# First layer of a graph network: a gathered chunk's products between the counting slots, table products two slots later, normalisation between one-hots

## What is computed

```
norm = deg_inv_sqrt[row] * deg_inv_sqrt[col]
msgs = x[row] * norm[:, None]
x = layernorm(x + segment_sum(msgs, col))            # first layer
h = relu(edge_attr_32 @ W1 + b1); w = (h @ W2 + b2).reshape(e, 4, 8, 8)
x = layernorm(x + (sums over edges of products of x[src], edge_attr_4 and w) + x @ si)   # second layer
```

## Time and profile before

| what | value |
|---|---|
| time, three runs | 3489.55 us median (3487.09 to 3490.99) |
| the profiled execution | 3488.94 us, of which the span of its instructions 3486.2 us |
| VectorE busy | 2974.5 us (85%) |
| TensorE busy (products) | 2796.1 us (80%) |
| GpSimd busy | 2464.9 us (71%) |
| ScalarE busy | 1433.7 us (41%) |
| first gathers of the first layer, last one's end | 105.3 us, 1281.8 us |
| first gather of the second layer | 1312.5 us |

### The profile page before, as it was taken

The page is one execution under the profiler, slowest core; times in us unless marked ns, Lnnn a source line. Parts: engine busy times, 40 slices in busy tenths (PEclk is TensorE's granted clock), DMA queues, the critical chain, the costliest instruction groups (busy, mean ns, idle before and its releaser), DMA issues.

```text
span 3486.2 us, 55367 instructions
## 1 busy us (share of the span) xinstructions
PE 2796.1 (80%) x17493; PEld 1893.0 (54%) x17493; DVE 2974.5 (85%) x6514; ACT 1433.7 (41%) x3154; POOL 2464.9 (71%) x2520
## 2 busy tenths in 40 slices
PE   5699999999999987777777787777778777877775
PEld 4477776777777764444444454444445444444443
DVE  8788888888888865988888889889889888988987
ACT  0788888888888863211121112111212121112211
POOL 0677776777777657777777777777777777777774
PEclk9999999999999997999898898999989998999988
DMA  2200000000000021111111111111111111111112
GB/s 50 29 14 14 13 14 13 14 14 13 12 14 14 13 34 22 31 27 28 27 31 27 27 27 31 27 27 28 30 27 28 27 31 27 27 28 27 31 27 34
DMA packets 181444, 85.57 MB, mean 25 GB/s; under 512 B 124024, under 2 KB 167608, under 8 KB 181176
## 3 DMA queue, kind: packets, MB, share of 16 engines
q0 software_dynamic: 79872, 41.05, 8.0%
q1 hardware_dynamic: 101304, 41.07, 5.2%
HBM read 77.13 MB, written 4.81 MB: 24 GB/s over the span
## 4 chain that ended last, share of the span: by engine, by line
POOL 39%; issue 17%; ACT 17%; PE 14%; DVE 12%; DVEq 1%; DMA 1%; POOLq 0%; SPq 0%; ACTq 0%
POOL xg L435 39%; ACT z_sb L476 9%; ACT q_sb L476 7%; PE ps L635 4%; PE ps L648 4%; PE ps L593 3%; DVE prod_all L1062 2%; DVE stage L1231 2%; PE ps L623 1%; DVE oh L949 1%; DVE prod_all L1221 1%; PE ps L739 1%; DVE sumT_all L1085 1%; DVE lane L1058 1%; DVE z_sb L841 1%
## 5 line engine op out<-in xcount | busy, mean ns | idle before, releaser
L435 POOL DMA_INDIRECT xg<-x_table,idx x1664 | 1602.5, 963 | 562.7 <-issue 531.4
L435 POOL DMA_INDIRECT xg<-scaled_x_table,idx x832 | 854.9, 1028 | 400.7 <-issue 374.5
L739 PE MATMUL ps<-w2t,hT 128*128 128x256 f32 x3328 | 899.8, 417 | 283.9 <-DVE prod_all L1221 278.9
L739 PEld LDWEIGHTS ps<-w2t,hT 128*128 128x128 f32 x3328 | 643.2, 204 | 735.7 <-issue 640.3
L635 PE MATMUL ps<-prod_all,lane 128*128 128x363 bf16 (+1 forms) x2496 | 792.5, 320 | 51.8 <-DVE prod_all L1062 35.0
L1062 DVE TENSOR_SCALAR prod_all<-wide_lane,key 128x363 bf16<-128x363 bf16 (+1 forms) x2496 | 730.4, 316 | 27.8 <-PE ps L635 23.0
L1231 DVE TENSOR_REDUCE stage<-prod_all 128x192 f32<-128x1536 f32 x416 | 724.0, 1741 | 0.2 <-issue 0.2
L523 ACT ACTIVATE hT<-ps,b 64x512 f32<-64x512 f32 x416 | 284.4, 684 | 932.7 <-PE ps L732 928.6
L476 ACT ACTIVATE q_sb<-ps 128x363 bf16<-128x363 f32 (+1 forms) x1248 | 504.7, 543 | 94.2 <-PE ps L635 87.8
L476 ACT ACTIVATE z_sb<-ps 128x363 bf16<-128x363 f32 (+1 forms) x1248 | 504.7, 543 | 85.1 <-PE ps L635 81.8
L1215 DVE TENSOR_TENSOR prod_all<-ps,stage 128x768 f32<-128x768 f32 x416 | 397.1, 955 | 143.6 <-PE ps L739 68.7
(11 more groups left out here) (128 smaller groups left out, 1528.5 us busy)
## 6 DMA issues: line engine op xcount, KB each, us to landing
efT<-in_efT SPq DMA_DIRECT2D x104, 256.0 KB
xg<-x_table,idx POOLq DMA_INDIRECT x1664
xg<-scaled_x_table,idx POOLq DMA_INDIRECT x832
sh<-in_sh SPq DMA_DIRECT2D x104, 32.0 KB
idx<-in_src SPq DMA_DIRECT2D x156, 8.0 KB
scaled_x_table<-q_sb SPq DMA_DIRECT2D x2, 784.0 KB, 7.6
x_table<-x_sb SPq DMA_DIRECT2D x7, 224.0 KB, 4.7
out_rows<-q_sb SPq DMA_DIRECT2D x6, 224.0 KB
```

Of the source, the lines that this page charges most:

```text
L435: pool.indirect_dma_start(rows[k][:, t, :], None, table, bass.IndirectOffsetOnAxis(ap=idx[k][:, t:t + 1], axis=0),).then_inc(s_g[layer][k] ...
L739: mm = pe.matmul(ps_w[j % 2][:, t, :], hT[j % 2][:, t * P:(t + 1) * P], w2t[:].rearrange("p c o i -> p (c o i)"), start=True, stop=True)
```

## The change

- **Products woven in.** `window_sums` takes a list of tiles. TensorE makes one product of chunk n-1 after every second slot of turn n, in the first 32 slots; those of the last two chunks come after the loop, in blocks. `slots_until` now gives even numbers.
- **Slots in pairs, more buffers.** `count_tile` waits only at even slots, for the pair; there are 4 PSUM banks for counts in place of 3 and `KR` = 8 spread buffers in place of 7 (`LEAD` stays 6).
- **Table products two slots later.** `apply_counts` is cut into 13 shares (`SHARES`) in place of 16, in slots 2 to 14 of the next range.
- **VectorE's order.** In turn n: the spreads of the first 34 slots, `add_gathered(n - 1)`, `one_hots(n + 1)`, `scale`, then the other spreads. Where a group is centred, its six instructions stand between six cuts of these other spreads (`centre_step`), one turn after TensorE has made its rows. The table adds that are left stand after the loop, ahead of the last chunk's add, as before.
- **Rows of a group.** `sums_to_rows` also waits for one-hots (`hots`), and stands behind the next turn's slots.
- **Lanes.** The bank of the lanes is taken by the fourth count bank. 128 lanes go to the end of bank 7, used by the chunk's one-hots alone; the table one-hots read `near_lanes` from SBUF.

```diff
@@
 RANGES = 3
 HR = 33
 HB = 14
-KR = 7
-LEAD = KR - 1
+KR = 8
+LEAD = 6
+SHARES = 13
+SPAN_SLOTS = 2 * TPC
 GB = 14
+STEPS = 6
 SLACK = 40
 WIDE = 512
 D = 32
@@
     assert KEY0 + 2 * P <= RW
 
     def slots_until(n):
-        return min(SLOTS, -(-SLOTS * (n + 1) // (CG - 1)))
+        return min(SLOTS, -(-SLOTS * (n + 1) // (2 * CG - 2)) * 2)
 
     def last_chunk_of(g):
         return CHUNKS - 1 if g == NG - 1 else min(CHUNKS - 1, math.ceil((GB * P * (g + 1) + SLACK) / RISE) - 1)
@@
         ps_sum = [ps[0:m, 6, 0:SPC * SW].rearrange("p (s w) -> p s w", s=SPC) for m in (D, DM)]
         ps_rows = ps[:, 7, 0:GB * D]
         ps_wide = [ps[0:m, 7, :] for m in (D, DM)]
-        ps_ring = [ps[:, b, 0:RW] for b in range(3)]
-        ps_lanes = ps[:, 3, 0:LW // 2]
-        lanes = ps_lanes.bitcast(BF16)
+        ps_ring = [ps[:, b, 0:RW] for b in range(4)]
+        ps_lanes = ps[:, 7, GB * D:GB * D + P // 2]
+        span_lanes = ps_lanes.bitcast(BF16)[:, 0:SW]
         ps_dense = [ps[0:D3, 4 + b, 0:TPC * TWIN] for b in range(2)]
         ps_low = ps[:, 7, 0:P]
         ps_piece = [ps[:, 3 + j % 4, 0:HB * D] for j in range(HBS)]
...
@@
                         mm.then_inc(s_dmm, 1)
             pe.matmul(ps_deg, zero_b[:], zero_b[:, 0:NP], start=False, stop=True).then_inc(s_degree, 1)
 
-            def window_sums(layer, rows, n):
+            def window_sums(layer, rows, n, tiles=range(TPC)):
 
                 k = n % 2
-                if layer == 0:
-                    pe.wait_ge(s_g[0][k], 16 * TPC * (n // 2 + 1))
-                else:
-                    pe.wait_ge(s_msg, 2 * n + 2)
-                pe.wait_ge(s_oh[layer], n + 1)
-                if n >= 1:
-                    pe.wait_ge(s_acc[layer], SPC * n)
-                for t in range(TPC):
+                for t in tiles:
+                    if t == 0:
+                        if layer == 0:
+                            pe.wait_ge(s_g[0][k], 16 * TPC * (n // 2 + 1))
+                        else:
+                            pe.wait_ge(s_msg, 2 * n + 2)
+                        pe.wait_ge(s_oh[layer], n + 1)
+                        if n >= 1:
+                            pe.wait_ge(s_acc[layer], SPC * n)
                     mm = pe.matmul(ps_sum[layer][:, t // TPS, :], rows[:, t, :], oh[layer][k][:, t, :],
                                    start=(t % TPS == 0), stop=(t % TPS == TPS - 1))
-                mm.then_inc(s_sum[layer], 1)
+                    if t == TPC - 1:
+                        mm.then_inc(s_sum[layer], 1)
 
             def wide_sums(layer, rows, n, landed):
 
...
-            def sums_to_rows(layer, g, gathered, dense):
-
+            def sums_to_rows(layer, g, gathered, dense, hots=0):
+
+                if hots:
+                    pe.wait_ge(s_oh[layer], hots)
                 pe.wait_ge(s_acc[layer], SPC * gathered)
                 if layer == 0:
                     pe.wait_ge(s_dacc, TPC * dense)
@@
             def count_tile(s):
                 g, t = s // TPC, s % TPC
                 a, b = spread_hi[g % RANGES]
-                if g % RANGES == 0:
-                    pe.wait_ge(s_ohlow, g // RANGES * TPC + t + 1)
-                pe.wait_ge(s_spread, s + 1)
-                if s >= 3:
-                    pe.wait_ge(s_evict, s - 2)
-                pe.matmul(ps_ring[s % 3][:, 0:(b - a) * TWIN], ohlow[:, t, :], spread[s % KR][:, 0:(b - a) * TWIN],
+                if s % 2 == 0:
+                    pe.wait_ge(s_spread, s + 2)
+                    if g % RANGES == 0:
+                        pe.wait_ge(s_ohlow, g // RANGES * TPC + t + 2)
+                    if s >= 4:
+                        pe.wait_ge(s_evict, s - 2)
+                pe.matmul(ps_ring[s % 4][:, 0:(b - a) * TWIN], ohlow[:, t, :], spread[s % KR][:, 0:(b - a) * TWIN],
                           start=True, stop=True).then_inc(s_count, 1)
 
             def apply_counts(g, share):
@@
                         pe.wait_ge(s_low_part, 1)
                     if g % RANGES == 0 and m >= 2:
                         pe.wait_ge(s_dacc, TPC * (m - 1))
-                for j in range((b - a) * share // TPC, (b - a) * (share + 1) // TPC):
+                for j in range((b - a) * share // SHARES, (b - a) * (share + 1) // SHARES):
                     mm = pe.matmul(ps_dense[m % 2], table[:, a + j, :], counts[g % 2][:, j, :, :].rearrange("p t w -> p (t w)"),
                                    start=(a + j == 0), stop=(a + j == NP - 1))
-                if share == TPC - 1:
+                if share == SHARES - 1:
                     mm.then_inc(s_apply, 1)
 
             def slot(s):
                 count_tile(s)
-                if s >= TPC:
-                    apply_counts(s // TPC - 1, s % TPC)
+                if s >= TPC and 2 <= s % TPC < 2 + SHARES:
+                    apply_counts(s // TPC - 1, s % TPC - 2)
 
             def pick_rows(tile):
                 pe.wait_ge(s_ohs, tile * 2 + 3)
@@
             with pe.If(all_near == 1):
                 pe.wait_ge(s_lanes, 1)
                 for n in range(CG):
-                    for s in range(slots_until(n - 1), slots_until(n)):
+                    first = slots_until(n - 1)
+                    for s in range(first, slots_until(n)):
                         slot(s)
-                    if n == CG - 1:
-                        for share in range(TPC):
-                            apply_counts(RANGES * CD - 1, share)
+                        if n >= 1 and s - first < SPAN_SLOTS and (s - first) % 2 == 1:
+                            window_sums(0, xg[(n - 1) % 2], n - 1, [(s - first) // 2])
+                    for g in range(NG):
+                        if turn_of(g) == n - 1:
+                            last = last_chunk_of(g)
+                            sums_to_rows(0, g, last // 2 + 1, (last + 1) // 2, min(CG, n + 2))
+                for share in range(SHARES):
+                    apply_counts(RANGES * CD - 1, share)
+                for n in range(CG - 2, CG):
                     window_sums(0, xg[n % 2], n)
-                    for g in range(NG):
-                        if turn_of(g) == n:
-                            last = last_chunk_of(g)
-                            sums_to_rows(0, g, last // 2 + 1, (last + 1) // 2)
                 for g in range(NG):
-                    if turn_of(g) >= CG:
+                    if turn_of(g) >= CG - 1:
                         last = last_chunk_of(g)
-                        sums_to_rows(0, g, last // 2 + 1, (last + 1) // 2)
+                        sums_to_rows(0, g, last // 2 + 1, (last + 1) // 2, CG)
...
@@
             dve.tensor_copy(low[:], low[:].bitcast(I32)).then_inc(s_key, 1)
             dve.tensor_copy(high, key[:].bitcast(I32)).then_inc(s_key, 1)
             dve.wait_ge(s_key, 4)
-            dve.tensor_copy(ps_lanes, lanes_b).then_inc(s_lanes, 1)
+            dve.tensor_copy(ps_lanes, lanes_b[:, -KEY0 // 2:P // 2 - KEY0 // 2]).then_inc(s_lanes, 1)
             dve.wait_ge(s_key, 6)
             dve.tensor_scalar(key[:], high, float(TWIN), float(KEY0), ALU.mult, ALU.add).then_inc(s_key, 1)
             dve.wait_ge(s_key, 7)
...
-                spans_of = lanes[:, -KEY0:SW - KEY0] if layer == 0 else ps_mlane
+                spans_of = span_lanes if layer == 0 else ps_mlane
                 dve.tensor_tensor(oh[layer][k], rel_b[:, c * TPC:(c + 1) * TPC].unsqueeze(2).to_broadcast([P, TPC, SW]),
                                   spans_of.unsqueeze(1).to_broadcast([P, TPC, SW]),
                                   ALU.is_equal).then_inc(s_oh[layer], 1)
@@
                 dve.wait_ge(s_node[layer], link(layer, dve.tensor_tensor(z_sq[:], z, z, ALU.mult)))
                 return dve.tensor_reduce(var[:, cols], z_sq[:], AX_X, ALU.add)
 
+            def centre_step(g, i):
+                z, cols = z_row[:], slice(g * GB, (g + 1) * GB)
+                if i == 0:
+                    dve.wait_ge(s_tr[0], g + 1)
+                    dve.tensor_tensor(z, ps_rows.rearrange("p (h f) -> p h f", f=D), spread_over(dinv, g),
+                                      ALU.mult).then_inc(s_ld[0], 1)
+                elif i == 1:
+                    dve.wait_ge(s_ld[0], g + 1)
+                    link(0, dve.tensor_tensor(z, z, blocks_of(x_sb, g), ALU.add))
+                elif i == 2:
+                    dve.wait_ge(s_node[0], links[0])
+                    link(0, dve.tensor_reduce(mean[:, cols], z, AX_X, ALU.add))
+                elif i == 3:
+                    dve.wait_ge(s_node[0], links[0])
+                    link(0, dve.scalar_tensor_tensor(out=z, in0=spread_over(mean, g), scalar=-1.0 / D, in1=z,
+                                                     op0=ALU.mult, op1=ALU.add))
+                elif i == 4:
+                    dve.wait_ge(s_node[0], links[0])
+                    link(0, dve.tensor_tensor(z_sq[:], z, z, ALU.mult))
+                else:
+                    dve.wait_ge(s_node[0], links[0])
```

(42 more changed lines are left out.)

6 lines of the change are left out of this document (3 added, 3 removed).

## The result

The changed kernel takes 3536.99 us (median of 4 runs, 3523.02 to 3540.51) against 3490.27 of the kernel before on the same chip: a ratio of 1.0129, with a 95% interval of 1.0109 to 1.0150. It is slower by about 47 us, where 3441 was forecast and 3515 was the top of the range.

The account below looks back on a forecast made before the run. VectorE was taken to hold the first layer's turn of 22.81 us; after the change GpSimd's gathers would, at 21.8, saving 1117 - 49 x 21.8 = 49 us: 3489.55 - 49 = 3441 us, range 3385 to 3515.

Parts of the forecast that it names:

- The wait for a chunk's sums: VectorE's add waiting for TensorE's products, 1.60 us a turn (73.6 us): claimed to go, with nothing in its place.
- the hidden table adds: End of first layer: 16 table adds ahead of the last chunk's add become hidden, about 10.5 us saved.
- Chunk 2's gather: Start of first layer: it waits for sums woven into turn 1, so starts at about 155 in place of 150.6.
- VectorE's turn: First-layer loop: 22.81 less 1.60, 0.35, 0.1 and 0.3 us saved, so 20.5 us.
- a chunk of gathers becomes the turn: First-layer loop: the bound moves from VectorE (20.5 us) to GpSimd's gathers, 21.3 to 22.2 us a chunk, taken as 21.8.
- the forecast's own GpSimd turn with gathers as before: GpSimd's chunk of 16 gathers at 1.025 us plus 0.304 us issue each: 21.3 us, the middle case's lower bound.
- up to the same again for changing between weights: TensorE's woven products: 2.29 us a turn as before, plus at most another 2.29; nothing was taken.
- it has 7 us a turn: TensorE's time per turn in which evictions or VectorE hold it, claimed to absorb the woven products' extra cost.
- rival B: Each turn's 10.4 us SBUF-only stretch: a gather held through it, turn 23.3 us, 25 us slower, 3515 us; chance 0.20.
- when GpSimd is late VectorE stops too: Argument against held gathers in the SBUF-only stretch: VectorE's stop frees the gather; no size given.
- 0.1 us a turn was taken as saved: Six normalisations: VectorE's wait for TensorE's rows goes, 0 to 0.25 us a turn, taken as 0.1.
- the forecast's own formula: End of first layer: last gather ends at 175.3 + 49 T, T the turn; saving 1117 - 49 T, 49 us at 21.8.

Follow-up runs that it names:

- y1: Changed kernel with a chunk's 16 products in one block behind the 16th slot, not woven: 3501.98 us, ratio 1.0048.
- x6: Changed kernel with the 16 products in one block behind slot 16 and table one-hots from PSUM (three count banks): 3461.20 us, ratio 0.9928.
- y2: Changed kernel, still woven, with table one-hots from PSUM and three count banks with waits slot by slot: 3504.14 us, ratio 1.0055.
- y4: Kernel before with only the table one-hots read from SBUF in place of PSUM: 3529.9 us, ratio 1.0127.
- v10: Kernel before with table one-hots from SBUF, made by a two-tensor comparison: 3569.01 us, ratio 1.0214.
- x4: Kernel before with only the table one-hots read from SBUF, on a slower chip (TensorE clock 0.75): ratio 1.0013 to the kernel before there.

## Why the prediction was wrong

**What held.** The wait for a chunk's sums is gone (4.5 us of 73.6). The end of the layer gives back 11.6 us, of which 10.5 were forecast for the hidden table adds. Chunk 2's gather was to start at 155, and starts at 155.07, but to the tenth this is luck: turn 1's slots start at 138.7, where the sum had 140.3, and its first 32 take 15.5 us, where the sum had 12.5 and 2.3. A one-hot from SBUF starts its spread after 0.16 us, for which 0.18 was estimated. The gathers' mean in the stretch was to be 1.04 to 1.08 and is 1.064, which makes GpSimd's chunk 16 x (1.064 + 0.304) = 21.9 us for a forecast of 21.8. VectorE's turn was put at 20.5 with nothing in its way; the first turns of y1 and x6 without a late gather or a normalisation take 20.2 to 21.3.

**What failed is the step from these two to the turn**: "a chunk of gathers becomes the turn", so 21.8. It is 23.60. GpSimd's average was right and yet isn't the turn; the turn is not the larger of two averages. Three terms are missing: the weaving (0.7 us a turn), the held gathers (0.7) and the normalisations (0.9). With 21.3, the forecast's own GpSimd turn with gathers as before, they make 23.6.

*The weaving's price on TensorE.* The text gave its bound ("up to the same again for changing between weights", 2.29 us a turn) and then took nothing, "it has 7 us a turn". The price is 3.3 us, above the bound, but it was mostly the second half that failed. The 7 us stand in no row. An estimate from the changed kernel's rows: 48.94 slots with a count product (0.155 us) and 2.04 table products (0.077 each) are 15.3 us, the block was 2.29, and 5.2 are left of 22.81, before the rows of a group. And they don't all lie in the 32 slots in which the products stand: there a pair takes 1.05 us, VectorE's alternation of one-hot and spread 0.78 (877.08 to 877.47 is one slot of it) and two spreads 0.47, so TensorE became the late engine. VectorE used up the lead of its spread buffers and then waited. It cost 0.67 us a turn beside the held gathers (22.93 of y1 to 23.60) and 0.76 without them (22.27 of x6 to 23.03 of y2): 35 and 43 us by the medians. Put with 0.7 us into the sum, it would have made the forecast 3475 and rival B 3550.

*Long gathers are not a mean.* Rival B had the place, the mechanism and nearly the price: y4, the kernel before with this one edit, has a turn of 23.67 (B: 23.3) and takes 42 us more (B: 25). I gave it 0.20, since 73 of 100 stretches caught no gather and since "when GpSimd is late VectorE stops too". The changed kernel has indeed only 54 us in long ones against 118 in y4; why fewer, the runs don't tell: y1, where no weaving stops VectorE, has only 66, and two of the changed kernel's eight end before VectorE stops at all. Still they cost 33 us, because they come in a few turns (158.30 and 178.25 in one chunk, then 209.61, each over 5.5 us). A chunk that is 6 us late with two buffers `xg` stops TensorE, as at 188.89, and then VectorE, whose spread buffers fill; the turns between, at 21.5 us, can't win it back, because VectorE's own work takes nearly as long. By the sums a mean of 1.064 spread over all turns would have been hidden (21.9 us a chunk); in a few gathers it isn't. No run spreads them out, so this last step is argued.

*A normalisation is not an average either.* VectorE's sum includes the normalisations, since it starts from the mean turn of 22.81, GpSimd's 21.3 has nothing of them, and the forecast then took GpSimd's. But six times VectorE is several us late, the sums are late with it, and GpSimd, with two buffers, stops: 0.93 us a turn in x6, on top of ordinary turns of 21.30. Nor did the changed order make a normalisation cheaper (7.6 us against 6.5 before), where 0.1 us a turn was taken as saved. That is why x6, with neither of the two costs, gains only 26 us: 1117 - 49 x (21.3 + 0.93) = 28.

**Against the marks set ahead.** Right: the add's wait, the mean gather. Wrong: TensorE waits for the gathers' DMA at five chunks in the stretch, not in most turns; GpSimd has 39.9 us of waits for sums by name, not only its own 0.30 us; the last gather ends at 1338.6, not at 1243 +- 25. Gathers of 5 us and more were named as the mark of B, and seven are there. The layer's end by the forecast's own formula, 175.3 + 49 x 23.60 = 1331.7, is 7 us short of the trace; one held gather, 8.26 us at 1291.59, belongs to the last chunk but one, behind the turns that the formula counts. The range missed because no case had both costs at once: each alone, 3502 and 3504 us, lies inside it.

**The rule on the ports.** In y4 one gather was held 9.91 us beside 30 spreads and 16 one-hots, yet 737 of y4's 832 gathers are at or under 1.2 us. The Trainium skill, "SBUF — State Buffer", section "SBUF: two separate sides", says that VectorE in a two-port mode, or with two SBUF inputs where the GpSimd operation reads SBUF, takes a shared pair of ports for a whole instruction; the gather reads its indices from SBUF (`idx`). By that rule v10's two-tensor one-hots had to hold the gathers as well, and the trace agrees (twenty-two over 3.3 us). It doesn't say why a gather is caught in one stretch and passes in the next. The traces tell a part: in y4, 14 of the 16 long gathers start between 0.10 us before and 0.51 us after the first instruction of a stretch of SBUF-only ones, but 23 others start there too and pass. In the changed kernel only three of the eight in the loop start so; the others start 0.95 to 1.83 us into a stretch.

**What stays open.** x6 has turns of 20.2 us at best and 22.27 on average. Beside the normalisations (their turns and the ones behind take 23.3 to 27.5 us), from turn 33 on ordinary turns, too, take 21.3 to 22.5, where the first eight take 20.2 to 21.8, which I haven't explained. Nor have I explained why eight gathers, not three or twenty, are caught in the changed kernel.

## What to carry to other kernels

Work that is woven into another engine's rhythm is paid in the slots where it stands, not out of the turn's spare time: compare the pair of slots on each engine, with the change of operands in it, and weave in groups (four behind eight slots were as good as one block, one behind two cost 35 us). A source moved from PSUM to SBUF can be cheaper for VectorE (254 against 269 ns) and dearer for the kernel, if it joins short stretches of SBUF-only work into one beside which GpSimd issues gathers. Where an engine has two buffers of lead, ask for the longest delay and how delays cluster, not for their mean; that holds for rare long work as well, such as a normalisation every seventh or eighth turn. A kernel that has slack at the place of a delay (here, on the slower chips) says nothing of what the delay costs where there is none.

## What the runs showed of the hardware

- An indirect gather of 128 rows, 0.94 us by itself, was held up to 11.29 us beside back-to-back VectorE instructions with all operands in SBUF, and in the two rows shown ended 0.55 and 0.7 us after the first idle 0.16 us of VectorE, or its first instruction with a PSUM operand. So it is for 14 of y4's 16 long gathers and all 22 of v10, 0.2 to 1.2 us after it; in the changed kernel two ended in the midst of back-to-back instructions. The two-tensor form held it no less than the one-tensor form.
- An fp32 product (128 x 32 weights, 76 columns) between bf16 products takes TensorE 0.35 us, in a block of its kind 0.143; a bf16 one in its place 0.23, of which 0.09 are ahead of its start.
- On three of the chips TensorE's mean granted clock was 0.75 and the same kernel took 1.53 times as long, more than the clocks' ratio (0.92 / 0.75 = 1.23): VectorE's instructions were as long as elsewhere, but it stood still 321.5 of 1050 us (x4) for a releaser that the profile calls remote.
